# Splitting each accumulating DMA of four odd token tiles into two of 512 KB, in an attention and selective-scan kernel

## What is computed

```python
# first layer: x -> layer norm -> q, k, v -> 16 heads of 32 -> softmax -> av
#   -> layer norm * (1 + scale(cond)) + shift(cond) -> silu -> out projection -> + x
# second layer, on its result:
x_in, z = split(xn @ in_proj_w.T)                  # 1024 channels each
u = silu(causal_conv4(x_in) + conv_b)
dt_r, B, C = split(u @ x_proj_w.T)                 # 64, 16, 16 columns
dt = softplus(dt_r @ dt_proj_w.T + dt_proj_b)
# for every channel d and every one of the 16 states n, over the tokens t:
h[t, d, n] = h[t-1, d, n] * exp(dt[t, d] * A[d, n]) + dt[t, d] * u[t, d] * B[t, n]
y[t, d] = sum_n h[t, d, n] * C[t, n] + u[t, d] * D[d]
out = x + gate(cond) * ((y * silu(z)) @ out_proj_w.T)
```

## Time and profile before

| | us |
|---|---|
| median of 3 runs | 7831.52 |
| lowest, highest | 7828.92, 7831.94 |
| the profiled execution | 7839.49 |
| its span | 7837.8 |
| TensorE busy in the span | 6334.3 (81%) |
| VectorE busy | 5962.5 (76%) |
| ScalarE busy | 4681.2 (60%) |
| GpSimd busy | 2845.7 (36%) |
| the GpSimd queue's packets, of 16 DMA engines' span | 21.7% |

### The profile page before, as it was taken

One profiled execution on the slowest core, in us unless ns is written; L12 is line 12 of the kernel. 1 busy time (PEld: TensorE's weight loads), 2 busy tenths in 40 slices (PEclk: granted clock), 3 DMA queues, 4 the chain that ended last, 5 costly groups with the idle time before them and its releaser, 6 DMA issues.

```text
span 7837.8 us, 136110 instructions
## 1 busy us (share of the span) xinstructions
PE 6334.3 (81%) x43168; PEld 4027.3 (51%) x43168; DVE 5962.5 (76%) x7305; ACT 4681.2 (60%) x6536; POOL 2845.7 (36%) x1390
## 2 busy tenths in 40 slices
PE   6996689966899678986889768887689876889768
PEld 2663447534575345743557435673356633466344
DVE  0768958699586995869958698686976779677895
ACT  2755647566475674746747466574666656566564
POOL 0006740077300872008800187003760047500574
PEclk9999899998999989999899899999899998999989
DMA  4114672157611675216741178312682136721367
GB/s 168 51 54 96 159 192 61 43 116 172 170 56 44 135 179 147 58 35 159 185 123 50 49 160 197 100 49 67 153 200 91 44 84 148 200 80 55 86 155 194
DMA packets 373295, 894.59 MB, mean 114 GB/s; under 512 B 46440, under 2 KB 46568, under 8 KB 371584
## 3 DMA queue, kind: packets, MB, share of 16 engines
q0 software_dynamic: 146720, 313.28, 21.7%
q1 hardware_dynamic: 207456, 539.10, 21.2%
q10 hardware_dynamic: 18432, 33.56, 1.3%
HBM read 474.21 MB, written 143.15 MB: 79 GB/s over the span
## 4 chain that ended last, share of the span: by engine, by line
PE 47%; issue 19%; POOL 16%; DVE 7%; DMA 5%; ACT 3%; DVEq 1%; POOLq 1%; ACTq 0%; SPq 0%
PE ps L1087 32%; POOL area_s L539 15%; PE ps L1188 8%; DMA area_acc<-area_w 4%; PE ps L1294 2%; PE ps L1137 2%; POOL area_acc L549 1%; DMA area_acc<-area_h 1%; DVE area_s L890 1%; DVE area_h L1008 1%; PE ps L1320 1%; DVE area_dt L996 1%; DVE area_u L899 1%; DVE area_dt L859 1%; PE ps L1263 1%
## 5 line engine op out<-in xcount | busy, mean ns | idle before, releaser
L539 POOL TENSOR_TENSOR area_s<-area_u,area_s 128x1024 f32<-128x1024 f32 x1024 | 2509.6, 2502 | 4134.0 <-DVE area_u L999 3841.6
L1008 DVE TENSOR_TENSOR_SCAN area_h<-ps,area_s 128x1024 f32<-128x1024 f32 x1024 | 2334.9, 2280 | 37.8 <-POOL area_s L539 28.0
L1294 PE MATMUL ps<-ident,area_h 128*128 128x128 f32 x8192 | 1217.0, 296 | 935.4 <-DVE area_acc L1018 580.6
L1294 PEld LDWEIGHTS ps<-ident,area_h 128*128 128x128 f32 x8192 | 997.5, 152 | 1625.3 <-DVE area_acc L1018 1032.9
L657 ACT ACTIVATE area_s<-area_s,negmax 128x1024 f32<-128x1024 f32 x1024 | 1177.3, 1150 | 633.4 <-DVE negmax L890 630.9
L890 DVE CUSTOM_DVE_ANT_0 area_s<-ps,area_dt 128x1024 f32<-128x1024 f32 x1024 | 1241.5, 1215 | 168.0 <-PE ps L1087 111.8
L731 ACT ACTIVATE ps<-area_dt,negA 128x1024 f32<-128x1024 f32 x1024 | 1145.4, 1119 | 320.6 <-DVE area_h L1008 160.2
L712 ACT ACTIVATE area_w<-ps,C_nat 128x512 f32<-128x512 f32 x992 | 680.0, 686 | 739.4 <-PE ps L1294 707.2
L1188 PE MATMUL ps<-ident,area_s 128*128 128x128 f32 x8192 | 1091.6, 277 | 0.0
L1087 PE MATMUL ps<-area_xT,area_w 128*128 128x512 f32 x2176 | 1014.1, 602 | 57.0 <-ACT k_stack L633 39.7
L1188 PEld LDWEIGHTS ps<-ident,area_s 128*128 128x128 f32 x8192 | 974.8, 144 | 149.7 <-issue 26.5
(11 more groups left out here) (112 smaller groups left out, 4995.4 us busy)
## 6 DMA issues: line engine op xcount, KB each, us to landing
area_acc<-area_w POOLq DMA_DIRECT2D x248, 1024.0 KB, 8.7
area_s<-b_rows SPq DMA_DIRECT2D x256, 512.0 KB, 4.7
q_stack<-qk_keep SPq DMA_DIRECT2D x520, 128.0 KB, 2.6
k_stack<-qk_keep SPq DMA_DIRECT2D x520, 128.0 KB, 3.0
qk_keep<-q_stack SPq DMA_DIRECT2D x144, 256.0 KB, 4.8
qk_keep<-k_stack SPq DMA_DIRECT2D x144, 256.0 KB, 5.2
area_w<-inT SPq DMA_DIRECT2D x16, 2048.0 KB, 11.1
z_keep<-z_st ACTq DMA_DIRECT2D x128, 256.0 KB, 4.2
```

What stands on the lines that cost most here:

```text
L539: pool.tensor_tensor(dbu[:, dl % 2, :], U[:, k // (NS * DL) * DL + dl, :], bb[:, q, :], ALU.mult).then_inc(s_dbu.sem, 1)
L1008: v.tensor_tensor_scan(out=hs[:, q, dl, :], data0=banks(2 * (dl % 2)), data1=dbu[:, dl % 2, :], initial=0.0, op0=ALU.mult, op1=ALU.add).th ...
L1294: last = nc.tensor.transpose(ps[:, 4 + n % 2, dl * P:(dl + 1) * P], hs[:, r % 2, dl, n * P:(n + 1) * P], ident[:, :])
```

## The change

Each state's accumulating DMA becomes two, of tiles 1 and 3 and of tiles 5 and 7, 512 KB each. Each half has a semaphore of its own, `s_ad[0]` and `s_ad[1]`, and waits only for its two evictions and for the same half of the state before. On GpSimd the first half is issued after the product of step 0, the second after that of step 2 (before, the one DMA after step 1); for the last two states the four halves follow after the last product, each when its evictions are done. ScalarE waits for the first half of the slot before tile 1 and for the second before tile 5. SP and VectorE wait for both semaphores where they waited for one. The first half's loop on GpSimd is written out.

```diff
--- before.py
+++ after.py
@@ -318,7 +318,7 @@
         s_ht = sig("h_transposed", DG * NS * NT, 2 * UN + NT + 1)
         s_acc = sig("acc_added", UN, 6 * UN)
         s_ev = sig("c_times_h_ready", UN, 8 * UN)
-        s_ad = sig("c_times_h_added", 16 * DG * NS)
+        s_ad = [sig(f"c_times_h_added{r}", 16 * DG * NS) for r in range(2)]
         s_zp = sig("z_projected", ZU, 1)
         s_zc = sig("z_copied", ZU)
         s_zs = sig("z_stored", 16 * ZU, 1)
@@ -442,7 +442,8 @@
                             parts_stored(b + 1)
                 first_stacks()
                 for half in (1, 0):
-                    sp.wait_ge(*s_ad.at(b, 16 * (DG * NS - 1 - half)))
+                    for hf in range(2):
+                        sp.wait_ge(*s_ad[hf].at(b, 16 * (DG * NS - 1 - half)))
                     sp.nop(nofuse=True)
                     sp.dma_start(wp[:, half * ND // 2:(half + 1) * ND // 2, :],
                                  opT[half * DI // 2:(half + 1) * DI // 2, :].rearrange("(k p) c -> p k c", p=P)
@@ -539,25 +540,21 @@
                     pool.tensor_tensor(dbu[:, dl % 2, :], U[:, k // (NS * DL) * DL + dl, :], bb[:, q, :], ALU.mult
                                        ).then_inc(s_dbu.sem, 1)
 
-                def add_part(r, slot):
-                    pool.wait_ge(*s_ev.at(b, (r + 1) * DL))
+                def add_part(r, slot, hf):
+                    pool.wait_ge(*s_ev.at(b, r * DL + 2 * (hf + 1)))
                     pool.nop(nofuse=True)
                     if not isinstance(r, int) or r:
-                        pool.wait_ge(*s_ad.at(b, r * 16))
+                        pool.wait_ge(*s_ad[hf].at(b, r * 16))
                         pool.nop(nofuse=True)
                     dg = r // NS if isinstance(r, int) else 0
-                    pool.dma_start(acc_odd[:, :, dg * 512:(dg + 1) * 512], part[slot], accum_op=ALU.add
-                                   ).then_inc(s_ad.sem, 16)
-
-                for q in range(2):
+                    pool.dma_start(acc_odd[:, 2 * hf:2 * hf + 2, dg * 512:(dg + 1) * 512],
+                                   part[slot][:, 2 * hf:2 * hf + 2, :], accum_op=ALU.add).then_inc(s_ad[hf].sem, 16)
+
+                for r in range(NS):
                     for dl in range(DL):
-                        inject(q, q, dl, q * DL + dl)
-                with pool.Fori(1, NS // 2) as i:
-                    for q in range(2):
-                        for dl in range(DL):
-                            inject(i, q, dl, q * DL + dl)
-                            if dl == 1:
-                                add_part(i * 2 + (q - 2), q)
+                        inject(r, r % 2, dl, r * DL + dl)
+                        if r >= 2 and dl % 2 == 0:
+                            add_part(r - 2, r % 2, dl // 2)
                 pool.wait_ge(*s_dbu.at(b, NS * DL))
                 pool.nop(nofuse=True)
                 load_next(b + 1)
@@ -565,10 +562,11 @@
                     for dl in range(DL):
                         at = r * DL + dl
                         inject(NS + r, r % 2, dl, NS * DL + at)
-                        if dl == 1:
-                            add_part(NS + r - 2, r % 2)
+                        if dl % 2 == 0:
+                            add_part(NS + r - 2, r % 2, dl // 2)
                 for r in (2 * NS - 2, 2 * NS - 1):
-                    add_part(r, 2 * (r % 2))
+                    for hf in range(2):
+                        add_part(r, 2 * (r % 2), hf)
                 pool.wait_ge(*s_da.at(b, UN))
                 pool.nop(nofuse=True)
                 load_mask(b + 1)
@@ -704,8 +702,8 @@
 
                     def scale_by_c(r, n, slot):
                         rr = dg * NS + r
-                        if n == 1 and (not isinstance(rr, int) or rr >= 2):
-                            act.wait_ge(*s_ad.at(b, rr * 16 - 16))
+                        if n % 4 == 1 and (not isinstance(rr, int) or rr >= 2):
+                            act.wait_ge(*s_ad[n // 4].at(b, rr * 16 - 16))
                             act.nop(nofuse=True)
                         act.wait_ge(*s_ht.at(b, rr * NT + (n + 1)))
                         act.nop(nofuse=True)
@@ -1058,7 +1056,8 @@
                         if dg + 1 < DG and n in (4, 6):
                             clip((dg + 1) * DL + (n == 6))
                 dve.wait_ge(*s_acc.at(b, UN))
-                dve.wait_ge(*s_ad.at(b, 16 * DG * NS))
+                for hf in range(2):
+                    dve.wait_ge(*s_ad[hf].at(b, 16 * DG * NS))
                 dve.wait_ge(*s_gbc.at(b, 16))
                 for s in range(NT + 2):
                     if s < NT:
```

## The result

The changed kernel is slower: 7858.31 us (median of 7 runs, 7850.06 to 7862.03) against 7831.52 us (7 runs, 7823.16 to 7837.41), a ratio of 1.0033 with an interval of 1.0022 to 1.0045. That is 27 us more, where 30 less were forecast, and it lies above the forecast's range of 7778 to 7848. The profiled execution took 7856.59 us, its span is 7854.9 (7837.8 before).

The account below looks back on a forecast made before the run. VectorE sets the first half's 11.36 us steady state, with GpSimd idle 0.71 us a state; TensorE is full near the second half's end. Terms 28 + 5 - 3 = 30 us less than 7831.52 gave 7802, range 7778 to 7848.

Parts of the forecast that it names:

- Part (3): GpSimd's second issue: 0.85 us of GpSimd per half, hidden in the steady state; 3 us lost in all, bounds 0 and 54.
- The threshold of 0.96: First half's steady state: GpSimd's cover is gone when an issue takes (11.36 - 9.44)/2 = 0.96 us of GpSimd.
- rival B: GpSimd becomes the bound, mainly in first-half states 2 to 15: 54 us lost, net +24, 7855; chance 0.18.
- The passage to the second half: Start of the second half, three products on end: the half issued between them pushes a scan about 0.4 us, 3 in all.
- Part (1): Last state at an element's end: halves land sooner, 3.5 us less per element, 28 in all; bounds 14 and 40.
- The gate row is late next: Element's end: the gating multiply also waits for the gate row, landing at 1091.6, so the gain is at least 1.7 us.
- the gate moves too: Element's end: SP issues weights and z 2 us earlier, so the gate row comes in at 1089 to 1090.
- half of the last addition runs in the half-empty stretch: Before 1080, DMA share 0.53 from 1075 to 1080: with it, the engines' work starts and ends about 3 us sooner.
- Rival C: Element's end hidden behind other DMAs, gate row as late as before: 1.7 x 8 = 14, net 11 less, 7820; chance 0.20.
- Part (2): Stall near 1057, late in the second half: TensorE gets back 0.6 us an element, 5 us in all; bounds 0 and 23.
- signs of being wrong: Issue over 1.03 us with scans waiting for GpSimd in every state, or the multiply's wait falling by less than 2 us.
- Part (4): The rest, ScalarE's, SP's and VectorE's extra waits and the first half's written-out GpSimd loop: nothing, 2 us either way.

Follow-up runs that it names:

- e4: Kernel before, with halves only for the last four states of an element (28 to 31), whole additions elsewhere: 7812.41 us, ratio 0.9973.
- e10: Kernel before, with halves for the last four states and the second half of the output weights loaded after z, x and gate row: 7791.88 us, 0.995.
- e8: Kernel before, with halves for the last four states and the gate row loaded before the output weights, to a free place: 7798.78 us, 0.9955.
- e7: Kernel before, whole additions, with only the gate row loaded early to a free place: 7829.61 us, 0.9998.
- e12: Kernel before, whole additions, with the gate row early and the second half of the output weights late: 7836.02 us, 1.0005.
- e1: Kernel before, whole additions, with only GpSimd's loop over the first half's states written out: 7832.92 us, 1.0004.

## Why the prediction was wrong, point by point

**Part (3) is the step that failed, and it turned the sign.** It took a half as 0.92 us recorded and 0.85 of GpSimd, by a straight line in the rows, between a lower bound of 0.65 and an upper of 1.29. A half records 1.19 on an idle engine and takes 1.13 in the stream. The line between a plain load of one row a partition and an addition of four was drawn through a step: the size asked for lay on the upper side of it. The threshold of 0.96 and the way to it were right, and 1.13 lies past it, so GpSimd became the bound where the prediction had its second issue hidden. The value was taken too near the cheap end: 0.11 us more than taken would have been enough for the cover to go, and the chance of rival B, 0.18, did not show how close that was.

**Rival B** had the mechanism and the first half of its place. Its price was 54 us, at 1.20 for a half; (4.25 + 0.36) x 8 = 37 was measured, at 1.13, and by its own scale that is (1.13 - 0.96) x 2 x 14 x 8 = 38. The rest of the 42 us that were lost is the passage, below. That B's sum, 7855, comes within 4 us of 7858 is luck in part: it set 54 us of loss against 30 of gain, and measured were 42 against 15, (0.80 + 1.07) x 8. Its assumption that a half costs what a whole does is near what was measured on an otherwise idle engine, 1.19 for two tiles against 1.27 for four; one tile, at 0.85, is not near it.

**The passage to the second half** was taken as 0.4 us an element; the scan there, in the timeline of the kernel after, waits for GpSimd:

```profile
883.84 2.29 DVE L1006 TENSOR_TENSOR_SCAN area_h<-ps,area_s 128x1024 f32<-128x1024 f32 x1 [0.50 <-POOL area_s L540]
```

where the same scan, at 878.98 before, followed without a wait. It lies in the stage of states 0 to 5 of the second half, which is 0.59 longer: the mechanism was right, the price is 5 us instead of 3. (The 0.36 before the first scan of the second half belong to state 15, with GpSimd still full.)

**Part (1), the end of an element, was mis-sized:** 3.5 us taken, 0.8 in after and 1.3 to 1.7 in e4. The gate row is late next, as forecast. Two steps of it failed.

The first is "the gate moves too". SP does issue the weights ahead of it earlier, 5.30 us before the last eviction ends instead of 2.63 (means of the elements). But before the x tiles and the gate row SP's program also waits for VectorE's last addition and for the last eviction (L463 to L466 of the kernel before), which neither the prediction nor the list of waits in "The kernel before" has. So the gate row is issued 1.30 us after the last eviction, where it was 1.34, and it then takes 11.5 us to land instead of 10.8.

The second is "half of the last addition runs in the half-empty stretch". In the changed kernel the first half of the last state is issued at 1077.59, and SP issues 1 MB of weights at 1078.15, 0.56 us behind it. The view of the DMA queues (packets, MB, share of the engines) for 1078.5 to 1082.5:

```profile
q1 hardware_dynamic: 312, 0.64, 63.7%
q0 software_dynamic: 1, 0.00, 0.3%
```

q0 is GpSimd's queue, q1 is SP's. The half had one packet while SP's loads issued behind it, the weights and from 1078.88 two z tiles, had 312. It lands at 1089.02, 11.4 us after its issue and 5.1 after that of the second half, so the two halves and the gate row pass through the engines together after all. e10 shows the other case: with the weights moved, the first half lands in 5.7 us.

The same view for 1081.6 to 1085.4 before, with the addition issued at 1080.24:

```profile
q1 hardware_dynamic: 372, 1.15, 102.5%
...
q0 software_dynamic: 1, 0.00, 0.3%
```

and for 1084 to 1089 after, with the half issued at 1083.91:

```profile
q1 hardware_dynamic: 351, 1.08, 58.0%
...
q0 software_dynamic: 234, 0.45, 48.5%
```

Before, the addition moved one packet in 3.8 us while the weights, z and x tiles, issued from 1076.87 on, were served. Its first packet comes 5.1 us after its issue; in a steady state, where the addition issued at 703.78 finds the engines free, it is 1.85 us. The prediction had scaled a crowd by bytes; here the loads issued just before the addition held it back, 5.1 us to the first packet against 1.85, and so did, after, the loads of SP that were issued 0.56 us and more behind the half. Rival C's price, 1.7, is about what the end is worth in e4. The rest, up to 4.4 us an element, came with moving the gate row and the weights on top of the halves (e8, e10); the gate row's move with whole additions gave nothing measurable (e7), nor did both moves (e12).

**Part (2), the stall near 1057,** was taken as 0.6 us an element. The scans come 2.06 us earlier, TensorE takes 1.09 of it back behind them, and 0.97 is left, 1.07 with the states just before. The bounds were 0 and 2.9; the cause was as forecast, the size taken a little too small.

**The signs.** Two of the prediction's own signs of being wrong came: an issue well over 1.03 us, with the first half's states bound by GpSimd, and a wait at the multiply that fell by 0.8 us, less than 2.

**Part (4), at nothing,** holds: e1 for the written-out loop (1.0004), and the second waits of ScalarE in the states that didn't move (47.44 us for states 5 to 9).

## What to carry to other kernels

Before a DMA is split, take the slack of the engine that issues it, per period, and set it against the price of a whole issue, not against a share of it: here 0.71 us of slack met two issues of 1.13 where one of 1.20 had been, 1.06 more, and 0.35 us a state was lost. Split only where somebody waits for the landing: halves in the last four of 32 states gave 0.9973 where halves in all gave 1.0033. When a landing ends a wait, look at what is issued close to it and at every wait that holds back the next one to land; with the splitting, putting them in order gave nearly as much again (0.995 with both), and without it nothing measurable.

## What the runs showed of the hardware that was not expected

- The price of GpSimd's issue of an accumulating DMA went by its form: 0.85 to 0.90 us for one 2 KB row in each of 128 partitions, 1.19 for two, 1.27 to 1.28 for three, 1.27 for four, 1.31 for four rows of 1 KB. In a full stream of products a half keeps the engine for 1.13 us, though its record there is 1.78 long and overlaps the next product.
- Two GpSimd additions waited behind transfers of SP's queue, one behind transfers issued before it, the other behind some issued shortly after it. Issued at 1080.24, behind 1 MB of weights and the z and x tiles, the first had 1 of the 373 packets between 1081.6 and 1085.4; issued at 1077.59, 0.56 us ahead of 1 MB of weights and 1.29 ahead of two z tiles, the second had 1 of the 313 packets between 1078.5 and 1082.5. With the engines free an addition's first packet came 1.85 us after its issue (703.78, before) and that of SP's weights 1.06 after theirs (1076.87), which would account for the overtaking; that is worked out, not tried.
- A full engine was all but missing from the table of waits: with GpSimd busy 110.00 of 110 us in the stretch from 690 to 800, the entry of the scans that wait for it was 10.7 us over the whole span, and with GpSimd busy 103.50 it was 28.0.
